# First rows' work in the setup, the last attention groups reordered, and a new due table in a Macaron transformer block

## What is computed

```python
x = x + 0.5 * ffn(layernorm(x))
x = x + attn(layernorm(x))
x = x + 0.5 * ffn(layernorm(x))
```

## Time and profile before

| | us |
|---|---|
| median of 3 timed runs (2241.99 to 2244.22) | 2242.98 |
| the profiled execution | 2243.43 |
| its span, first to last instruction | 2241.4 |
| mean granted TensorE clock, share of full | 0.964 |

### The profile page before, as it was taken

How to read it: one execution, slowest core, us unless ns; L and a number is a source line. 1 busy time by engine, 2 the same in 40 slices (tenths; PEclk the granted TensorE clock), 3 DMA queues, 4 the chain that set the end, 5 groups by cost and what they waited for, 6 DMA issues and landing times. The chain is left out here.

```text
span 2241.4 us, 39700 instructions
## 1 busy us (share of the span) xinstructions
PE 1894.6 (85%) x13634; PEld 779.9 (35%) x13634; DVE 1663.2 (74%) x3657; ACT 1725.1 (77%) x2598; POOL 1350.0 (60%) x1427
## 2 busy tenths in 40 slices
PE   2477888899999898998998889999999899988845
PEld 2233433343423232443332433343332343332212
DVE  8898988688846888888856798888955786845324
ACT  3456787888887788787878788888879889888842
POOL 3788676566734666776744666776744755733213
PEclk9799999999999999999999999999999999999977
DMA  4134444224211443334321335333421423411102
GB/s 111 27 63 92 74 77 72 56 61 83 47 42 36 66 78 78 76 54 86 57 50 25 73 57 109 72 54 71 79 52 23 75 44 73 78 46 26 30 10 45
DMA packets 477493, 136.17 MB, mean 61 GB/s; under 512 B 458222, under 2 KB 477038, under 8 KB 477294
## 3 DMA queue, kind: packets, MB, share of 16 engines
q1 hardware_dynamic: 477294, 133.65, 31.6%
HBM read 11.96 MB, written 8.39 MB: 9 GB/s over the span
## 5 line engine op out<-in xcount | busy, mean ns | idle before, releaser
L1306 ACT ACTIVATE probs<-psum_s 128x1024 f32<-128x1024 f32 (+3 forms) x1280 | 1075.0, 899 | 120.2 <-PE psum_s L1583 102.9
L1601 PE MATMUL psum_o<-probs,v_sb 128*32 128x512 f32 (+3 forms) x5120 | 573.8, 543 | 34.0 <-DVE o_sb L1466 13.9
L1544 PE MATMUL shared<-w_gu_T,xT 128*128 128x480 f16 (+1 forms) x2304 | 505.8, 368 | 88.4 <-DMA xT<-x 48.4
L1583 PE MATMUL psum_s<-q_stack,k_stack 64*128 64x512 f16 (+3 forms) x2560 | 393.5, 354 | 102.7 <-ACT probs L1306 89.6
L1544 PEld LDWEIGHTS shared<-w_gu_T,xT 128*128 128x128 f16 x2304 | 210.9, 99 | 368.1 <-issue 94.0
L1557 PE MATMUL shared<-w_down_T,hT 128*128 128x256 f16 x2176 | 268.4, 279 | 34.1 <-DMA hT<-h 17.9
L1583 PEld LDWEIGHTS psum_s<-q_stack,k_stack 64*128 64x128 f16 x2560 | 96.7, 94 | 517.6 <-ACT probs L1306 418.2
L1216 POOL TENSOR_SCALAR_AFFINE_SELECT probs<-probs 128x512 f32<-128x512 f32 x256 | 177.4, 699 | 150.7 <-ACT probs L1306 149.5
L1183 POOL TENSOR_TENSOR hq<-grid,qscale 128x704 f32<-128x704 f32 x128 | 180.9, 1413 | 132.0 <-DVE grid L1397 132.0
L1230 ACT ACTIVATE hq<-shared,tanh_scale 128x240 f32<-128x240 f32 (+1 forms) x384 | 171.8, 457 | 109.0 <-PE shared L1544 108.0
L1557 PEld LDWEIGHTS shared<-w_down_T,hT 128*128 128x128 f16 x2176 | 208.1, 100 | 103.1 <-issue 37.0
(11 more groups left out here) (132 smaller groups left out, 2308.8 us busy)
## 6 DMA issues: line engine op xcount, KB each, us to landing
xb<-L_attn_x SPq DMA_DIRECT2D x16, 512.0 KB, 4.2
out<-xb SPq DMA_DIRECT2D x16, 512.0 KB, 2.9
xT<-x SPq DMA_TRANSPOSE x128, 3.1
hT<-h SPq DMA_TRANSPOSE x128, 3.5
k_stack<-st SPq DMA_TRANSPOSE x64, 3.3
q_stack<-st SPq DMA_TRANSPOSE x64, 3.3
k_stack<-L_ffn_w_down SPq DMA_DIRECT2D x1, 704.0 KB, 4.1
k_stack<-L_ffn_w_gate SPq DMA_DIRECT2D x1, 480.0 KB, 6.1
```

The lines of the kernel that those rows point to most:

```text
L1306: nc.scalar.activation(probs[:, s % 3, 2 * u:2 * u + 2, q0:CHUNK], psum_s[u][:, :, q0:CHUNK], ACT.Exp, scale=HD ** -0.5 / QK_SCALE ** 2).t ...
L1544: last = nc.tensor.matmul(bank(e)[:, 0:2 * (hi - lo)], xs[:, x, t % 2, k, :], w_gu_T[:, w, k, 2 * lo:2 * hi], start=n == 0, stop=n == len( ...
L1583: last = nc.tensor.matmul(psum_s[u][:, j, q0:CHUNK], k_stack[half, at, h, kt % NTC * P:(kt % NTC + 1) * P], q_stack[half, c % 2, h, q0:CHU ...
L1601: last = nc.tensor.matmul(psum_o[at:at + VD, q0:CHUNK], v_sb[:, kt // NTC % SLOTS * NTC + kt % NTC, 2 * g + u, :], probs[:, s % 3, 2 * u + ...
```

## The change

- **Setup.** The stages of pass 0 for chunk 0 (`stats`, `rstd`, and all x stages of both pairs, the set `LEAD`) are issued inside the setup block, between the weights' passes. The plan gives them no cost, and the statistics of chunks 1 to 4 now need the last of their transposes. Chunk 0's rows are loaded before the attention weights. The setup's transposes use four PSUM banks (`psum_s`) and the peaks `psum_o`; `low_parts(1)` goes ahead of `top(1)`. The stage loops become functions that take a list of stages; the stages' own instructions are as before.
- **Steps.** The last 112 steps go (chunk 14, group 0), chunk 15's four groups, (chunk 14, groups 1 to 3). Stages that name the chunk before use `attended_before`.
- **Buffers.** In pass 2 the last pair of chunk 14 uses the buffers of passes 0 and 3.
- **Table.** All 97 rows of `DUE` have new numbers.

```diff
 DUE = {
...
-    "scores0": (51036, 56397, -196427, -622579, -1092511, -607229, -678187, -519771, 94889, -122901, 190114, 612982, 125829, 130406, 417537, 305463, 767114, 257430, 1332951, 955512, 921375, 875516, 1082811, 1379526, 1103812, 1433364, 345782, 649310, 845031, 1531024, 876757, 1114797),
+    "scores0": (-1318830, -1793542, -1008586, -1303101, -2384464, -279011, -4442987, -3625236, 760151, -740536, -3288309, -4367719, -3876240, -1935504, -2723935, -3910578, -1032720, -2116373, -464964, -1218375, 1551318, -1248033, -2281142, 127906, -773114, -716956, -904750, 384501, 1042695, 808639, -605993, -1176187),
...
 }
...
+X_STAGES = ("norm_a", "scale_x", "divide_x", "square_x", "grid_x", "points_x", "dequant_x", "high_x", "low_x", "turn_x")
+LEAD = {("stats", 0, 0), ("rstd", 0, 0), *((stage, "x", 0, p) for stage in X_STAGES for p in range(NTC // 2))}
...
     out, diagonals = [], 0
-    for c in range(BATCHES * NCH):
+    end = BATCHES * NCH - 1
+    turns = [(c, g) for c in range(end - 1) for g in range(NG)]
+    turns += [(end - 1, 0), *((end, g) for g in range(NG)), *((end - 1, g) for g in range(1, NG))]
+    for c, g in turns:
         mine = c % NCH
...
-def rings_of(pas):
-
-    own = pas in (1, 2)
+def rings_of(pas, p):
+
+    own = pas == 1 or pas == 2 and p != NTC * (BATCHES * NCH - 1) // 2 - 1
     return "pu" if own and PU else "xu", "p16" if own and P16 else "x16", "pT16" if own and PT16 else "xT16"
...
+        lead = name in LEAD
         family, c, i, n = at
         first, last = DUE[family][2 * c:2 * c + 2]
         weight = COST[name[0]] if weight is None else weight
+        if lead:
+            weight = lands = 0
...
-        roots(("stats", 0, c), [("load", c) if c >= XC else None])
+        roots(("stats", 0, c), [("load", c) if c >= XC else ("turn_x", "x", 0, NTC // 2 - 1) if c else None])
...
-            banks = [psum_s[0][:, 0], psum_s[0][:, 1], psum_s[1][:, 0], psum_s[1][:, 1],
-                     psum_o, *shared[0:BANKS - 1]]
+            banks = [psum_s[0][:, 0], psum_s[0][:, 1], psum_s[1][:, 0], psum_s[1][:, 1]]
-            peaks = shared[BANKS - 1]
+            peaks = psum_o
...
+                    pool.wait_ge(fills_done, 2)
+                    gpsimd_stages(pool, first["rstd"])
+                    quantised_weights(0)
+                    gpsimd_stages(pool, first["divide_x"])
+                    quantised_weights(1)
+                    gpsimd_stages(pool, first["dequant_x"])
+                    gpsimd_stages(pool, first["low_x"])
+                    quantised_weights(2)
...
+                    scaled_weights(ROUNDS[0])
+                    scaled_weights(ROUNDS[1])
+                    vector_stages(dve, first["stats"])
+                    scaled_weights(ROUNDS[2])
                     grid_points(0)
+                    vector_stages(dve, first["scale_x"])
                     top(0)
                     grid_points(1)
                     powers(0)
+                    for p in range(NTC // 2):
+                        vector_stages(dve, [first["grid_x"][p], first["points_x"][p]])
                     attention_peaks()
                     low_parts(0)
                     grid_points(2)
+                    low_parts(1)
                     top(1)
-                    low_parts(1)
...
+                        if i == 2:
+                            scalar_stages(act, first["norm_a"])
...
+                    scalar_stages(act, first["square_x"])
                     for n, (m, srcs, height, high, low) in enumerate(moves):
+                        if n == sum(move[0] == 0 for move in moves):
+                            scalar_stages(act, first["high_x"])
...
```

More of the change, by code:

```diff
@@ L488, in whole_plan @@
                 norm = ("norm_heads", "x", *pair)
-                add(norm, "vector", of_pair("norm_heads", *pair), [("head_stats", c)], [(rings_of(2)[0], pair)])
+                add(norm, "vector", of_pair("norm_heads", *pair), [("head_stats", c)], [(rings_of(*pair)[0], pair)])
                 halved(*pair, norm)
@@ new lines, in macaron_kernel @@
+        qk_read = sem("qk_read")
+        roped_ready = sem("roped_ready")
+        qk_n_ready = sem("qk_n_ready")
+        hi_ready = sem("hi_ready")
+        lo_ready = sem("lo_ready")
+        scores_full = sem("scores_full")
+        exp_done = sem("exp_done")
+        masked = sem("masked")
+        values_done = sem("values_done")
+        turned = [sem(f"turned{i}") for i in range(ST)]
+        o_copied = sem("o_copied")
+        plan = whole_plan()
+        order = plan.order()
+        FIRST_OF = {engine: [e for e in order[engine] if e in LEAD] for engine in order}
@@ new lines, in macaron_kernel @@
+        REST = {engine: order[engine][len(FIRST_OF[engine]):] for engine in order}
+        assert not any(e in LEAD for engine in order for e in REST[engine])
+        first = {kind: [e for engine in order for e in FIRST_OF[engine] if e[0] == kind]
+                 for kind in ("stats", "rstd", *X_STAGES)}
+        BANK = plan.bank
+        STAT = plan.ring["stats"]
+        GU_OF = plan.ring["gu"]
+        user = {r: {n: u for u, n in plan.ring[r].items()} for r in plan.ring}
+        QUANT = ordinals(order["vector"], ("quant_h", "scale_x"))
@@ new lines, in squares, with points, halves, landed @@
+        def squares(kind, key):
+            return bank(("square_x", "x", *key))[:, 0:2 * C] if kind == "x" else grid[:, GU_OF[kind, *key] % GU, :]
+        def points(kind, key):
+            return buffers(kind, key)[0] if kind == "x" else grid[:, GU_OF[kind, *key] % GU, :]
+        def halves(kind, key):
+            return (x16 if kind == "x" else h16)[:, slot_of(kind, key, 1)]
+        def landed(kind, key):
+            r = ring(kind, key, 1)
+            return (x_turned if kind == "x" else h_turned)[slot_of(kind, key, 1)], \
+                16 * (plan.ring[r][key] // plan.sizes[r] + 1)
@@ new lines, in last_low, with bank, full, read @@
+        def last_low(kind, key):
+            before = before_in(ring(kind, key, 0), key)
+            return LOW["low_" + kind, kind, *before] + 1 if before else None
+        def bank(e):
+            return shared[BANK[e][0]]
+        def full(e):
+            return bank_full[BANK[e][0]], BANK[e][1] + 1
+        def read(e):
+            return bank_free[BANK[e][0]], BANK[e][1] + 1
+        def wait_read(engine, stages):
+            last = {}
+            for e in stages:
+                last[BANK[e][0]] = max(last.get(BANK[e][0], 0), BANK[e][1] + 1)
+            for i, n in last.items():
+                engine.wait_ge(bank_free[i], n)
@@ L1621, in macaron_kernel, with _ @@
-        run(whole_plan())
+        with nc.Block() as block:
+            @block.sync
+            def _(sp):
+                sync_stages(sp, REST["sync"])
+                sp.wait_ge(out_stored, 16 * BATCHES * NCH)
+            @block.gpsimd
+            def _(pool):
+                gpsimd_stages(pool, REST["gpsimd"])
+            @block.scalar
+            def _(act):
+                scalar_stages(act, REST["scalar"])
+            @block.vector
+            def _(dve):
+                vector_stages(dve, REST["vector"])
+            @block.tensor
+            def _(pe):
+                tensor_stages(pe, REST["tensor"])
```

1243 lines of the change are left out of this document (598 added, 645 removed), and 134 rows, old and new, of the table DUE.

## The result

The changed kernel takes 2248.81 us (median of 20 runs, 2241.08 to 2254.07); the kernel before took 2243.39 beside it (20 runs). The ratio is 1.0023, with an interval of 1.0014 to 1.0032: slower by 5.4 us, just over the 4.5 us that the prediction took for what can be told from no change. I forecast 2220, in a range from 2190 to 2245, and faster. The profiled execution took 2249.77, its span is 2247.9.

What follows compares the result with a forecast made beforehand. It took the time as head and tail bound by dependent chains plus a packed middle of fixed PE work. 2243.4 less 8 (head), 6.5 (end order), 3.3 (buffers) and 5 (table) gave 2220.6, said as 2220, range 2190 to 2245.

Steps and rivals of the forecast that it cites:

- the term of the table: Packed middle, attention from 200 us: new table numbers take 5 us off, a twentieth of the exps' 102.9 us of waits.
- The head: Setup to first hidden matmul: moving chunk 0's first stages into the setup saves 8 us, bounds 3 and 11.
- my 6.5 + 3.3: End of the kernel: 6.5 us saved by the new group order, 3.3 by the last pair's other buffers.
- my bounds of 71 less and 56 more: Table's bounds in the middle: PE 93.2% busy throughout gives 71 us less, 87.3% gives 56 more.
- Rival D: Middle: early scores make PE stand, its share falls to 88.5%, slower at 2254 us; chance 0.13.
- half a point the sign of a wrong forecast: Middle: PE's share forecast at 90.0%; a move over half a point either way would show the forecast wrong.
- The end order: Attention's end: chunk 14's last three groups after chunk 15's save net 6.5 us, bounds 5 lost and 11 won.
- The two terms: End order: 11 us off attention as MLP work moves behind it, less 4.5 us of collisions on chunk 14's chain.
- The price of 4.5 on chunk 14's chain: Behind attention: some 25 chain instructions find VectorE occupied four times in ten, costing 4.5 us.
- the 0.6 that I took: Attention's end: about 60% of chunk 15's MLP falls behind attention, taking 0.6 x 18.5 = 11 us off it.
- The buffers: Tail: with its own x buffers the last pair's projections follow the first pair's 3.3 us earlier, bounds 0 and 3.3.
- Rival B: Setup and behind attention: every moved GpSimd pass stops VectorE for its whole length, giving 2233 us; chance 0.12.

Runs made afterwards that it cites:

- jitter_a: The changed kernel with each number of the new table moved at random by up to 20,000, under 1% of a row's spread; 2353.96 us, ratio 1.0491.
- head_back: The changed kernel with chunk 0's first stages issued at the start of the second block instead of inside the setup; 2258.54 us, ratio 1.0062.
- head_ring: The kernel before with its old lists, chunk 0's first stages in the setup and the last pair in the other buffers; 2240.12 us, ratio 0.9992.
- refit_end: Changed setup, end order and buffers, with the old table except chunks 12 to 15, fitted anew to the planner's own costs; 2233.57 us, ratio 0.9965.
- end_back: The changed kernel, new table numbers kept, with the last attention groups in the old sequence; 2268.64 us, ratio 1.0114.
- ring_only: The kernel before with its old lists, only chunk 15's last pair in pass 2 using the other x buffers; 2240.38 us, ratio 0.9989.

## Why the prediction was wrong

**The failed step is the term of the table.** I took "5 us less, by the nearest row, the waits themselves", a twentieth of a wait. The marks show 21.0 us more instead, from 203 to 1853, where the lists are the only thing that changed. That is 26 us off. The head is 5.5 us off as well (8 forecast, 2.5 left at the mark of 203), and the end came out 2.1 us better than my 6.5 + 3.3 (8.4 up to the last values and 3.5 behind them). Together this is the 29 us between the forecast and the chip. By the prices of single runs the table's loss is 24.5 (9.7 for the head in the new lists, 6.5, 2.9, and 5.4 lost in sum), or 15 if the head is taken at the 0.5 that it gave in the old lists: the parts don't add, so no one figure is the table's. All of these lie inside my bounds of 71 less and 56 more, and so it was the choice, not the bounds.

I argued from how the numbers differ (scores earlier), which says nothing: jitter_a differs from the new table in nothing one can read, and loses 105 us. Nor was the reading right, that exps stay or go later: exp0 for chunk 3 goes earlier too, by 2.3 million. Two better arguments were at hand. One is the planner's own length, 22 us less by its costs, hardly any of it in the middle. The other is that a packed order found against the planner's costs depends on what the chip takes beyond them. Such a row was there, the queue's 1.2 to 1.4 us for a transpose against `turn_x=200`, and the prediction reads no row of SP. The edit of the transposes accounts for 12 of the 27 us; the cause of the rest is open.

**Rival D** had the sign and nearly the size (2254), and I gave it 0.13. Its mechanism holds in part: PE stands more, but the scores' waits grew by 6.4 us only. In the worst stretch 17 of 26.5 us are idle time of PE, and 9.5 are slower matmuls. Its measure, PE's share, misled as mine did. The share moved by 0.2 points, and I had called half a point the sign of a wrong forecast; the 9.5 us of slower matmuls hid in it.

**The head: the start was right, what it is worth was not.** The setup's last instruction starts at 65.96 and ends at 66.11, the first hidden matmul starts at 66.81; I had 66.7 and 67.2. What should arrive of it was to be read from VectorE's idle time, and I took 7 us of it and then 8 in all. VectorE's busy time between 47.9 and 81.3 us is 26.51, so only 3.4 us more than before, and at the mark of 203 PE is 2.5 us ahead. head_back has 19.38 there, 7.1 less than the changed kernel: without the head the new lists would be behind the old ones. With the old lists the same move gives 0.5.

**The end order: agrees in size, and its own part is not shown.** Net 6.5 forecast; 6.5 measured between head_ring and refit_end, which also has a new fit there. The two terms were off. Chunk 15's downs stand in the gap behind attention in the changed kernel:

```profile
2164.07 2.02 PE L1222 MATMUL shared<-w_down_T,hT 128*128 128x256 f16 x17 [0.46 <-DMA hT<-h]
2171.14 3.78 PE L1222 MATMUL shared<-w_down_T,hT 128*128 128x256 f16 x17 [5.06 <-DMA hT<-h]
2175.36 1.47 PE L1283 MATMUL shared<-w_proj_T,xT 128*128 128x256 f16 x12 [0.44 <-DMA xT<-x]
2177.20 1.47 PE L1283 MATMUL shared<-w_proj_T,xT 128*128 128x256 f16 x12 [0.37 <-DMA xT<-x]
2182.20 3.57 PE L1222 MATMUL shared<-w_down_T,hT 128*128 128x256 f16 x17 [3.53 <-DMA hT<-h]
```

PE does 12.96 us of work there, against 6.08. The price of 4.5 on chunk 14's chain was not paid: last values to first hidden matmul takes 35.9 us in the changed kernel and 36.1 in end_back, whose chain has no such neighbour. But less of the MLP falls behind attention than the 0.6 that I took: 6.9 us more of PE's work there, of some 24 that an MLP has (twelve hidden parts of 1.3 to 1.4 us and four downs of 2.0), 0.3 of it. And refit_end gains 4.6 us up to the last values where I had 11.

**The buffers: right in the trace.** The projections start 1.84 us apart instead of 5.99. 3.3 was forecast; ring_only gave 2.9, with an interval from none to 5.4.

**Rival B** did not come. By it the setup would have ended 6.4 us later than I had it, near 73, and it ended at 66.11; the chain behind attention was not held up either. Its row was misread, too. The prediction says that the trace agrees in kind and not in size with the lock that the Trainium skill describes (SBUF — State Buffer, "SBUF: two separate sides"). But one more pair of rows of the kernel before belongs to the earlier trace rows:

```profile
25.89 1.74 DVE L825 SCALAR_TENSOR_TENSOR probs<-probs,k_stack 128x1536 f32<-128x1536 f32 x1
31.98 2.81 POOL L762 TENSOR_TENSOR k_stack<-k_stack,hq 128x1536 f32<-128x1536 f32 x1 [1.69 <-DVE k_stack L826]
```

The same GpSimd pass takes 2.81 us elsewhere. Its 4.56 at 25.73 are 1.75 more, the length of VectorE's pass at 25.89, which was not slowed. It ends at 30.29, 2.63 us after VectorE's next pass starts at 27.66, and that one grew by 2.49. So each waited until the other had ended, to within 0.15 us, and the trace agrees in size too. What B had wrong is that every moved pass of GpSimd meets one of VectorE's.

## What to carry to other kernels

Where an order comes out of a search over a table, the table belongs to one structure. Cost a structural change only together with its new fit, and read the planner's own length first: here it told ten of eleven differences within 15 us, a loss of 112 among them, and missed the one that mattered by 27. Before trusting a fit compare each cost the planner uses, DMA queues included, with the trace; here the transposes, counted at a sixth of their time on the queue or less, held 12 of the 27 us by all that plain copies change. Change a fitted program as locally as you can: the old numbers for all but the last four chunks turned a loss of 5 us into a gain of 8. And compare traces at equal work, not by an engine's busy share.

## What the runs showed of the hardware

A transposing DMA holds SyncE's queue for 1.23 to 1.41 us, a plain one of the same bytes for 0.46 (xT, hT) or 0.6 to 0.7 (q and k). After a wait of 4.55 us the same 12 matmuls took 4.67 us instead of 2.60, at a granted clock of 0.55 instead of 1.00, so this wait cost almost half as much again behind it. A VectorE pass and a GpSimd pass that met waited for one another: 1.76 us became 4.25, and 2.81 became 4.56. What remains open is the other half of the 27 us, and which of queue time, landing time and packets counts; a run that changes one of them alone was not made.
